# State scan of a fused GNN and Mamba kernel: where the exponentials lie, and which engine multiplies by B

## Chip, core and metric

The kernel runs on one core of a Trainium2 chip. The metric is the device time of one execution in microseconds (us). A core has TensorE (PE), VectorE (DVE), ScalarE (ACT) and GpSimd (POOL), which work in parallel and meet by semaphores, and a sync engine (SP) that issues transfers.

## What is computed

Two graph layers stand one behind the other. The second holds a selective state-space model (Mamba) over 4096 rows, with 256 channels and 16 states:

```python
dA = jnp.exp(dt[:, :, None] * A[None])
dBu = dt[:, :, None] * B[:, None, :] * u[:, :, None]

def step(hst, inp):
    dAt, dBut, Ct = inp
    hst = dAt * hst + dBut
    return (hst, hst @ Ct)
_, ys = lax.scan(step, jnp.zeros((D_INNER, D_STATE), h.dtype), (dA, dBu, C))
y = ys + u * D_skip
y = y * jax.nn.silu(z)
return y @ w_out
```

## The kernel before

Stage A, the first layer, comes first and is not touched. Stage B works on 8 tiles of 512 rows (`TILES`, `TILE`), numbered `b`. The 256 channels are two halves (`H`) of 128 partitions, so one state's sequence for a tile is 128 x 1024 elements, two halves side by side. Tile `b` has a **window** of 16 steps `n`, one for each state; in it the engines also prepare tile `b+1` (the "front") and finish tile `b-1` (the "tail"). Windows 0 and 1 and windows 6 and 7 are written out, 2 to 5 come out of a loop of two passes over two windows. Window 7 has a code of its own (`window_last`).

For a state `k` of a window:

- ACT writes the exponentials dA, one instruction for each half (L834), to SBUF (`dA`, 4 slots) or, for states in `IN_BANK` and the first half, to a PSUM bank (`dA_bank`, M1 being bank 3, or bank 6).
- dBu is the product of `dtu` and B. DVE makes it from a row of B that PE spread over the partitions in PSUM (`spread_B`, L1393, then L1111, into `dBuV`); for the states of `POOL`, GpSimd makes it from a copy of B that a transfer (`load_B`, L780, two states at a time into `b_sb`) has spread in SBUF (L546, into `dBuP`).
- DVE scans. A **banked** state takes two instructions, the first half from the bank (L1124), the second from SBUF (L1127); their start values are an operand. A **carried** state takes one instruction over both halves (L1132); its start value must stand in column 0 of the dBu tile, and ACT puts it there (`dBuP<-state`, L844), which DVE waits for (`start_set`). `AT['act_start']` = 1 puts that copy of state `k` into ACT's step `k+1`, behind the exponentials of that step.
- DVE multiplies by C (L1139, `pr`), from a bank that PE spread C into (`spread_C`, L1402), and PE adds the result up by transposing it into `yT` (`sum_state`, L1420).

Each engine runs its instructions in the order of its own list. `AT` is a table that says in which step `n` of an engine's list a piece of front or tail stands: `act_ax` (`front_ax`, L680, copies the finished product with the adjacency to SBUF), `act_g` (`front_relu`, L684), `act_fs` (`front_stats`, L691 to L698, mean and variance of the four row groups), `act_hn`, `act_skip` (`skip_term`, L759), `act_y` (`tail_copy`, L767, two copies that PE's sum of the next tile waits for), `pool_rs` (the power of -1/2 on GpSimd, L529). Within a step of ACT's list stand, in this order: the copy of the state four behind, the two exponentials, the start value, the load of B, the front, the skip term, the copies of y. DVE's step `n` holds the product with B of state `n`, the scan of state `n-1` and the product with C of state `n-2`. PE's step `n` holds the spread of B for state `n+1` (where DVE needs it), the sum of state `n-3`, a piece of the front and the spread of C for state `n-1`.

Of the kernel before, what the change touches and what calls it, by code (L numbers as in the profile page):

```python
# [7 lines left out]
ALU = mybir.AluOpType  # L8
ACT = mybir.ActivationFunctionType
# [16 lines left out]
S = 16  # L26
# [10 lines left out]
AT = dict(pool_rs=5, pool_tail_rs=13, dve_dt=14, act_hn=5, act_hT=6, act_silu=11, act_bc=13,
          act_sp=14, act_exp=14, act_ts=13, act_tail=15, dve_bc=11, dve_sp=14, dve_gate=1, pe_gcn=2, pe_gtr=3, pe_tr=6,  # L40
          pe_z=9, pe_dbc=10, pe_dt=11, pe_turn=2, pe_out=9, act_b0=15, act_ax=2, act_g=2, act_fs=4,
          act_start=1, act_skip=2, act_y=3)
FILL = (1, 1, 6, 1, 0, 0, 0, 9, 8)
CONV = (0, 0, 0, 0, 0, 0, 0, 4, 4, 0, 0, 0, 0, 0, 0, 0)
PLAN = (2, 4, 1, 2, 3, 3, 3, 0, 0, 0, 0, 2, 3, 3, 3, 3)
AHEAD = sum(PLAN[AT['pe_gcn']:])
C_IN_O = (0, 2, 4, 6)
POOL = (1, 2, 3, 4, 5, 6, 7, 9, 11, 13, 15)
IN_BANK = (1, 2, 3, 4, 5, 6)
CARRIED = tuple(k for k in range(S) if k not in IN_BANK)  # L50
B_LOADS = ((1, 2), (3, 4), (5, 6), (7, 9), (11, 13), (15,))
B_LOAD_AT = {3: 2, 5: 3, 8: 4, 11: 5}
POOL_AFTER = {n: 2 if n <= 7 else 3 for n in POOL}
SUM_AFTER = 3
LATE = (S - 2, S - 1)

# [1 line left out]
def gnn_mamba(nc, x, adj, x2, eps1, eps2, W1, b1, W2, b2, Wm, bm, gcn_w, gcn_b, ln_g, ln_b, w_in, conv_w,  # L58
              conv_b, w_xp, w_dt, b_dt, A_log, D_skip, w_out, out):
    POOL_B = POOL  # L60
    ctx = ExitStack()
    with ctx:  # L62
# [50 lines left out]
        state = sb("state", [P, S, H])  # L113
# [22 lines left out]
        B = ExitStack()  # L136
# [37 lines left out]
        bank = [yT[:, 0:TILE], yT[:, TILE:]]  # L174
# [101 lines left out]
        turns = {5: [("C", 1), ("C", 3), ("C", 5), ("C", 7), ("C", 8), ("B", 12), ("C", 11), ("C", 12), ("C", 14)],  # L276
                 6: [("B", 8), ("B", 10), ("C", 9), ("C", 10), ("B", 14), ("C", 13), ("C", 15)]}
        bank_of = {it: k for k in turns for it in turns[k]}
        dA_bank = {1: M1, 2: bank[6], 3: M1, 4: bank[6], 5: bank[6], 6: bank[6]}

        def spread_bank(kind, n):
            return M0 if (kind, n) == ("B", 0) else bank[4] if kind == "C" and n in C_IN_O else bank[bank_of[kind, n]]
# [1 line left out]
        def dve_slot(n, par):  # L284
            return (n - nB(n) + NVB * par) % 2

        def pool_slot(n, par):
            return (nB(n) + NPB * par) % 2

        def dBu(n, par):  # L290
            return dBuP[pool_slot(n, par)] if n in POOL_B else dBuV[dve_slot(n, par)]

        LAST = TILES - 1
        last_dA = ((bank[7], bank[6]), (M0, M1))
# [122 lines left out]
        def _(pool):  # L417
# [121 lines left out]
            def window(b, par, tail, front):  # L539
                for n in range(S):  # L540
                    if n in POOL_B:
                        load = nB(n) // 2
                        pool.wait_ge(b_in[load % 2], 16 * (len(B_LOADS) // 2 * b + load // 2 + 1))
                        wait(pool, scanned, S * b + n - POOL_AFTER[n] + 1 if n > 1 else S * b)
                        pool.wait_ge(dtu_ready, b + 1)
                        nc.gpsimd.tensor_tensor(dBu(n, par)[:, :, 1:], dtu[par][:, :, :],  # L546
                                                b_sb[load % 2][:, nB(n) % 2:nB(n) % 2 + 1, :].to_broadcast([P, H, TILE]),
                                                ALU.mult).then_inc(dBu_by_pool, 1)
                    if front and n == AT['pool_rs']:
                        front_rs(b + 1)  # L550
                    if tail and n == AT['pool_tail_rs']:
                        tail_rs(b - 1)
# [29 lines left out]
        def _(act):  # L582
# [233 lines left out]
            def window(b, par, tail, front):  # L816
                for n in range(S):
# [18 lines left out]
                    first = n - AT['act_start']
                    for k in range(first, S if n == S - 1 else min(first + 1, S - 1)):
# [98 lines left out]
        def _(dve):  # L936
# [167 lines left out]
            def window(b, par, tail, front):  # L1104
                for n in range(S + 2):
# [99 lines left out]
        def _(pe):  # L1205
# [390 lines left out]
```

## Time and profile before

| | us |
|---|---|
| median of 3 runs (1086.82 to 1090.28) | 1087.23 |
| the profiled execution's own time | 1086.18 |
| its span, first to last instruction | 1084.6 |
| DVE busy | 995.6 |
| PE busy | 971.7 |
| ACT busy | 559.5 |
| POOL busy | 337.6 |

The rows further down come from that one execution. Their first number is the start in us from the beginning of the span, the second the duration. What stands in brackets is idle time of the engine ahead of the row and what ended it. Since instructions of one engine overlap by some tenths of a us, the pace of a row is the distance to the next start, not the duration.

### The profile page before, as it was taken

The numbers are of one execution on the slowest core, as the hardware profiler recorded it, in microseconds if no ns is written. First come the engines' busy times: TensorE is split into PE (matmuls) and PEld (weight loads), VectorE is DVE, ScalarE is ACT, GpSimd is POOL, SyncE is SP. The second block draws the span as 40 slices with busy tenths as digits, with TensorE's granted clock in tenths as the row PEclk, the third lists the DMA queues.
The fourth block names the chain that finished last, engine by engine and source line by source line (L and its number), as shares of the span: only waits on it lengthen the run. The fifth ranks groups of instructions, "written<-read, shape, count | busy, mean of one in ns | idle before, by whom it ended". The sixth has DMA issues, their size and how long they took to land. (4 is left out here: it accounts for less than half of the span.)

```text
span 1084.6 us, 13272 instructions
## 1 busy us (share of the span) xinstructions
PE 971.7 (90%) x4134; PEld 671.6 (62%) x4134; DVE 995.6 (92%) x735; ACT 559.5 (52%) x1110; POOL 337.6 (31%) x228
## 2 busy tenths in 40 slices
PE   2889999999999999999998998989989999877665
PEld 2667777777777777634554564655646556445554
DVE  5989999999999999771999999999999999999996
ACT  3343343434343434225583875767847758477342
POOL 5450202020202021100532634426335263253652
PEclk9899999999999999999999999999999999988566
DMA  9999999999999999963825535365164452211200
GB/s 255 259 267 312 332 310 347 324 345 321 355 324 343 324 341 343 225 213 140 309 98 212 213 103 195 142 215 213 61 223 165 175 179 83 97 68 68 99 1 20
DMA packets 190396, 233.72 MB, mean 215 GB/s; under 512 B 8880, under 2 KB 164592, under 8 KB 175760
## 3 DMA queue, kind: packets, MB, share of 16 engines
q1 hardware_dynamic: 105936, 163.60, 46.3%
q10 hardware_dynamic: 80896, 60.57, 20.8%
q0 software_dynamic: 3520, 9.04, 2.8%
q8 instruction: 18, 0.29, 0.1%
q14 instruction: 26, 0.21, 0.1%
HBM read 170.00 MB, written 63.18 MB: 215 GB/s over the span
## 5 line engine op out<-in xcount | busy, mean ns | idle before, releaser
L958 DVE STREAM_TRANSPOSE at<-rows 128x1024 f32<-128x1024 f32 x136 | 267.8, 2011 | 21.9 <-DMA rows<-in_adj 7.5
L546 POOL TENSOR_TENSOR dBuP<-dtu,b_sb 128x1024 f32<-128x1024 f32 x77 | 182.9, 2376 | 282.1 <-DVE dtu L1074 115.1
L1223 PE MATMUL yT<-ah,xh 128*128 128x512 f32 x512 | 212.3, 415 | 34.8 <-DVE al L966 27.0
L599 ACT ACTIVATE ah<-at 128x2048 fp32r<-128x2048 f32 x64 | 122.6, 1915 | 211.4 <-PE yT L1223 196.1
L1310 PE MATMUL bank<-adjc,xm 128*128 128x512 f32 x448 | 206.0, 595 | 0.8 <-ACT axT L680 0.8
L1223 PE MATMUL yT<-al,xh 128*128 128x512 f32 x512 | 202.1, 395 | 0.0
L1223 PE MATMUL yT<-ah,xl 128*128 128x512 f32 x512 | 201.9, 394 | 0.0
L1420 PE MATMUL yT<-ident,pr 128*128 128x128 f32 x1008 | 147.4, 294 | 37.7 <-DVE pr L1139 31.2
L1420 PEld LDWEIGHTS yT<-ident,pr 128*128 128x128 f32 x1008 | 128.1, 152 | 67.9 <-DVE pr L1139 45.6
L834 ACT ACTIVATE dA<-dt,A_sb 128x512 f32<-128x512 f32 x182 | 122.6, 711 | 43.0 <-DVE dt L1071 43.0
L1139 DVE TENSOR_TENSOR pr<-hs,bank 128x1024 f32<-128x1024 f32 x112 | 134.3, 1199 | 11.2 <-PE bank L1402 11.0
L1223 PEld LDWEIGHTS yT<-ah,xh 128*128 128x128 f32 x512 | 97.8, 191 | 67.3 <-DVE al L966 34.0
L966 DVE TENSOR_TENSOR al<-at,ah 128x2048 fp32r<-128x2048 f32 x57 | 129.2, 2266 | 4.8 <-ACT ah L599 4.8
L1310 PEld LDWEIGHTS bank<-adjc,xm 128*128 128x128 f32 x448 | 81.2, 191 | 78.1 <-issue 77.3
L1223 PEld LDWEIGHTS yT<-ah,xl 128*128 128x128 f32 x512 | 97.7, 191 | 23.2 <-issue 3.6
L1223 PEld LDWEIGHTS yT<-al,xh 128*128 128x128 f32 x512 | 97.5, 190 | 21.2
L1132 DVE TENSOR_TENSOR_SCAN hs<-dA,zero,dBuV 128x1026 f32<-128x1026 f32 x35 | 83.0, 2371 | 1.8 <-ACT dA L834 1.4
L1132 DVE TENSOR_TENSOR_SCAN hs<-dA,zero,dBuP 128x1026 f32<-128x1026 f32 x35 | 83.9, 2397 | 0.0
L504 POOL TENSOR_TENSOR al<-at,ah 128x2048 fp32r<-128x2048 f32 x7 | 32.3, 4612 | 157.2 <-ACT ah L599 157.2
L1402 PE MATMUL bank<-bc,sel 128*128 128x512 f32 x112 | 73.9, 660 | 3.5 <-DVE pr L1139 1.8
L1127 DVE TENSOR_TENSOR_SCAN hs<-dA,state,dBuP 128x512 f32<-128x512 f32 x42 | 62.7, 1493 | 0.0
L1344 PE MATMUL bank<-hT,w_cv_sb 128*128 128x512 f32 x128 | 58.3, 599 | 0.2 <-ACT hT L713 0.2
(187 smaller groups left out, 1190.0 us busy)
## 6 DMA issues: line engine op xcount, KB each, us to landing
adjT<-at SPq DMA_DIRECT2D x56, 1024.0 KB, 7.5
adjc<-adjT SPq DMA_DIRECT2D x56, 1024.0 KB, 5.3
rows<-in_adj SPq DMA_DIRECT2D x152, 256.0 KB, 8.3
rows<-in_adj ACTq DMA_DIRECT2D x136, 256.0 KB, 8.7
b_sb<-b_dram ACTq DMA_DIRECT2D x37, 512.0 KB, 4.9
xm<-in_x SPq DMA_DIRECT2D x4, 512.0 KB, 10.7
res<-in_x POOLq DMA_DIRECT2D x8, 256.0 KB, 7.1
mid<-xn POOLq DMA_DIRECT2D x8, 256.0 KB, 7.9
```

Source lines behind the costliest of these rows:

```text
L546: nc.gpsimd.tensor_tensor(dBu(n, par)[:, :, 1:], dtu[par][:, :, :], b_sb[load % 2][:, nB(n) % 2:nB(n) % 2 + 1, :].to_broadcast([P, H, TILE ...
L599: nc.scalar.activation(ah[c % 2][:, :], at[c % 2][:, :, :].rearrange("p m t -> p (m t)"), ACT.Copy)\
L834: nc.scalar.activation(dA_bank[n][:, :] if n in IN_BANK and h == 0 else dA[n % NDA][:, h, 1:], dt_[par][:, h, :], ACT.Exp, scale=A_sb[:, h ...
L958: last = nc.vector.transpose(dst.rearrange("p m (g i) -> p g m i", i=32), src.rearrange("p g (i m) -> p g m i", i=32))
L966: nc.vector.tensor_tensor(al[c % 2][:, :], at[c % 2][:, :, :].rearrange("p m t -> p (m t)"), ah[c % 2][:, :], ALU.subtract).then_inc(chunk ...
L1127: nc.vector.tensor_tensor_scan(hs[k % NHS][:, 1, 1:], dA[k % NDA][:, 1, 1:], dBu(k, par)[:, 1, 1:], state[:, k, 1:2], ALU.mult, ALU.add).t ...
L1132: nc.vector.tensor_tensor_scan(flat[0], flat[1], flat[2], zero[:, :], ALU.mult, ALU.add)\
L1139: nc.vector.tensor_tensor(pr[k % NPR][:, :, :], hs[k % NHS][:, :, 1:], spread_bank("C", k)[:, :].unsqueeze(1).to_broadcast([P, H, TILE]), ...
L1223: last = mm(acc[k][:, :], w[:, b, :], v[c % 2][:, cols], start=(b == 0 and j == 0), stop=(b == KB - 1 and j == 2))
L1310: last = mm(accB[:, :], xm[:, b, :], adjc[c % NADJ][:, m, :], start=(b == 0), stop=(b == KB - 1))
L1402: mm(spread_bank("C", n)[:, :], sel[:, S + n:S + n + 1].to_broadcast([P, P]), bc[par][:, :], start=True, stop=True).then_inc(C_spread, 1)
L1420: m = mm(yT[:, DI * q + P * h:DI * q + P * h + P], src[:, h, P * q:P * q + P], ident[:, :], is_transpose=True, start=first and h == 0 and ...
```

## The change

Three of the banked states, 0, 2 and 4, read the exponentials of both halves from banks (M1 and bank 6). States 5, 6, 7 and 8 read the first half from bank 6. States 1 and 3, which were banked, become carried. GpSimd makes the product with B of state 8 too (12 of 16), so DVE and PE's spread are left with 0, 10, 12 and 14; the pairs of loads and the dBu slots are set anew. The product's wait is a table (`POOL_BEHIND`: the scan that product `n` stands behind). The power moves from behind product 5 to behind product 4, `front_stats` from ACT's step 4 to 3, the skip term from 2 to 1, the copies of y from 3 to 2.

```diff
-AT = dict(pool_rs=5, ... act_fs=4,
-          act_start=1, act_skip=2, act_y=3)
+AT = dict(pool_rs=4, ... act_fs=3,
+          act_start=1, act_skip=1, act_y=2)
...
-POOL = (1, 2, 3, 4, 5, 6, 7, 9, 11, 13, 15)
-IN_BANK = (1, 2, 3, 4, 5, 6)
+POOL = (1, 2, 3, 4, 5, 6, 7, 8, 9, 11, 13, 15)
+WHOLE_IN_BANK = (0, 2, 4)
+IN_BANK = (0, 2, 4, 5, 6, 7, 8)
...
-B_LOADS = ((1, 2), (3, 4), (5, 6), (7, 9), (11, 13), (15,))
-B_LOAD_AT = {3: 2, 5: 3, 8: 4, 11: 5}
-POOL_AFTER = {n: 2 if n <= 7 else 3 for n in POOL}
+B_LOADS = ((1, 2), (3, 4), (5, 6), (7, 8), (9, 11), (13, 15))
+B_LOAD_AT = {3: 2, 5: 3, 6: 4, 10: 5}
+POOL_BEHIND = {1: -1, 2: -1, 3: 1, 4: 1, 5: 3, 6: 3, 7: 5, 8: 6, 9: 7, 11: 8, 13: 10, 15: 12}
...
-        dA_bank = {1: M1, 2: bank[6], 3: M1, 4: bank[6], 5: bank[6], 6: bank[6]}
+        dA_bank = {(0, 0): M1, (0, 1): bank[6], (2, 0): M1, (2, 1): bank[6], (4, 0): bank[6], (4, 1): M1,
+                   (5, 0): bank[6], (6, 0): bank[6], (7, 0): bank[6], (8, 0): bank[6]}
...
         def dBu(n, par):
-            return dBuP[pool_slot(n, par)] if n in POOL_B else dBuV[dve_slot(n, par)]
+            if n in (2, 5):
+                return dBuV[1]
+            if n in POOL_B:
+                return dBuP[0 if n in (1, 4, 7, 9, 13) else 1]
+            return dBuV[dve_slot(n, par)]
...
-                        wait(pool, scanned, S * b + n - POOL_AFTER[n] + 1 if n > 1 else S * b)
+                        wait(pool, scanned, S * b + POOL_BEHIND[n] + 1)
...
-                        if n == 2:
-                            wait(act, C_multiplied, S * b)
-                        elif n == 3:
-                            act.wait_ge(half_scanned, len(IN_BANK) * b + 1)
-                        elif 4 <= n <= 6:
-                            act.wait_ge(half_scanned, len(IN_BANK) * b + (2 if n == 4 else n - 1))
+                        if n in (2, 4):
+                            act.wait_ge(scanned, S * b + n - 1)
+                        elif n in (5, 6, 7, 8):
+                            act.wait_ge(half_scanned, len(IN_BANK) * b + n - 2)
                         for h in range(H):
-                            nc.scalar.activation(dA_bank[n][:, :] if n in IN_BANK and h == 0 else dA[n % NDA][:, h, 1:], dt_[par][:, h, :], ACT.Exp,
+                            if n == 0 and h == 1:
+                                wait(act, C_multiplied, S * b)
+                            nc.scalar.activation(dA_bank[n, h][:, :] if (n, h) in dA_bank else dA[n % NDA][:, h, 1:], dt_[par][:, h, :], ACT.Exp,
...
-                            nc.vector.tensor_tensor_scan(hs[k % NHS][:, 1, 1:], dA[k % NDA][:, 1, 1:], dBu(k, par)[:, 1, 1:],
-                                                         state[:, k, 1:2], ALU.mult, ALU.add).then_inc(scanned, 1)
+                            nc.vector.tensor_tensor_scan(hs[k % NHS][:, 1, 1:], dA_bank[k, 1][:, :] if k in WHOLE_IN_BANK else dA[k % NDA][:, 1, 1:],
+                                                         dBu(k, par)[:, 1, 1:], state[:, k, 1:2], ALU.mult, ALU.add).then_inc(scanned, 1)
```

ACT's list ahead of the change, from the copies of y in step 3 to the exponentials of state 5 (`bank3` and `bank6` are PSUM, `dA0` to `dA3` the SBUF slots, `hn` and `ve` the statistics):

```order
L767 ACTIVATE y<-yT 128x512 [waits y_turned] x2
L821 ACTIVATE state<-hs0 128x2 [waits scanned]
L834 ACTIVATE bank6<-dt1,A_sb 128x512 [waits half_scanned,scanned]
L834 ACTIVATE dA0<-dt1,A_sb 128x512
L691 ACTIVATE hn,mr<-bank2 128x128 [waits h_turned,f_mean_scaled,g_turned]
L691 ACTIVATE hn,mr<-bank2 128x128 x3
L695 ACTIVATE hn,sq<-bank2,mr 128x128 [waits f_mean]
L695 ACTIVATE hn,sq<-bank2,mr 128x128 x3
L698 ACTIVATE ve<-sq,eps_ln 128x4 [waits f_squares]
L821 ACTIVATE state<-hs1 128x2 [waits scanned]
L834 ACTIVATE bank6<-dt1,A_sb 128x512 [waits half_scanned,scanned]
L834 ACTIVATE dA1<-dt1,A_sb 128x512
```

ACT's list with the change, from the exponentials of state 3 to the start value of state 3 (the last row):

```order
L837 ACTIVATE dA3<-dt1,A_sb 128x512 [waits scanned]
L837 ACTIVATE dA3<-dt1,A_sb 128x512
L783 DMA b_sb0<-b_dram 128x1024 [waits dBu_by_pool]
L694 ACTIVATE hn,mr<-bank2 128x128 [waits h_turned,f_mean_scaled,g_turned]
L694 ACTIVATE hn,mr<-bank2 128x128 x3
L698 ACTIVATE hn,sq<-bank2,mr 128x128 [waits f_mean]
L698 ACTIVATE hn,sq<-bank2,mr 128x128 x3
L701 ACTIVATE ve<-sq,eps_ln 128x4 [waits f_squares]
L824 ACTIVATE state<-hs0 128x2 [waits scanned]
L837 ACTIVATE bank6<-dt1,A_sb 128x512 [waits scanned]
L837 ACTIVATE bank3<-dt1,A_sb 128x512
L847 ACTIVATE dBuP1<-state 128x2 [waits state_kept,scanned]
```

The statistics now stand ahead of the exponentials of state 4, and behind these there is a start value for state 3, which had none.

DVE's list ahead of the change, from the second half of state 6 to the scan of state 7:

```order
L1127 SCALAR_TENSOR_TENSOR hs2<-dA2,state,dBuP1 128x512
L1139 TENSOR_TENSOR pr1<-hs1,bank5 128x1024 [waits summed,scanned,C_spread]
L1107 REGISTER_ALU
L1111 TENSOR_TENSOR dBuV1<-dtu0,bank6 128x2x512 [waits scanned,B_spread]
L1116 ISA
L1118 REGISTER_ALU [waits dA_ready]
L1130 REGISTER_ALU [waits C_multiplied,state_kept,dBu_by_pool]
L1132 SCALAR_TENSOR_TENSOR hs3<-dA3,zero,dBuP0 128x1026 [waits start_set]
```

With the change, from the same second half of state 6:

```order
L1129 SCALAR_TENSOR_TENSOR hs2<-dA2,state,dBuP1 128x512
L1141 TENSOR_TENSOR pr1<-hs1,bank5 128x1024 [waits summed,scanned,C_spread]
L1119 ISA
L1121 REGISTER_ALU [waits dA_ready]
L1127 SCALAR_TENSOR_TENSOR hs3<-bank6,state,dBuP0 128x512 [waits C_multiplied,state_kept,dBu_by_pool]
L1129 SCALAR_TENSOR_TENSOR hs3<-dA3,state,dBuP0 128x512
```

The product with B of state 8 is gone from DVE, and state 7 is two half scans.

## Rows read from the trace of the kernel before

**Rows 1.** The stretch of one window: PE, PEld, DVE, ACT, POOL busy, clock, DMA.
```profile
728.63:798.80 70.17, 65.38 (x296) 40.77 (x295) 68.68 (x51) 47.38 (x123) 29.69 (x15) 1.00 0.47 170
```
**Rows 2.** Timeline of DVE in that window.
```profile
728.63 1.21 DVE L1139 TENSOR_TENSOR pr<-hs,bank 128x1024 f32<-128x1024 f32 x1
729.77 1.22 DVE L1111 TENSOR_TENSOR dBuV<-dtu,bank 128x1024 f32<-128x1024 f32 x1
731.34 2.35 DVE L1132 TENSOR_TENSOR_SCAN hs<-dA,zero,dBuV 128x1026 f32<-128x1026 f32 x1 [0.36 <-ACT dA L834]
733.61 1.20 DVE L1079 TENSOR_TENSOR yg<-yT,sz 128x1024 f32<-128x1024 f32 x1
...
737.15 1.19 DVE L1139 TENSOR_TENSOR pr<-hs,bank 128x1024 f32<-128x1024 f32 x1
738.26 1.27 DVE L1124 TENSOR_TENSOR_SCAN hs<-bank,state,dBuP 128x512 f32<-128x512 f32 x1
739.45 1.31 DVE L1127 TENSOR_TENSOR_SCAN hs<-dA,state,dBuP 128x512 f32<-128x512 f32 x1
740.69 1.19 DVE L1139 TENSOR_TENSOR pr<-hs,bank 128x1024 f32<-128x1024 f32 x1
...
744.24 1.19 DVE L1139 TENSOR_TENSOR pr<-hs,bank 128x1024 f32<-128x1024 f32 x1
...
750.08 2.25 DVE L1127 TENSOR_TENSOR_SCAN hs<-dA,state,dBuP 128x512 f32<-128x512 f32 x1
...
764.33 1.22 DVE L1139 TENSOR_TENSOR pr<-hs,bank 128x1024 f32<-128x1024 f32 x1 [0.47 <-PE bank L1402]
...
772.89 1.22 DVE L1139 TENSOR_TENSOR pr<-hs,bank 128x1024 f32<-128x1024 f32 x1 [0.57 <-PE bank L1402]
```
**Rows 3.** Timeline of PE in that window.
```profile
737.01 1.04 PE L1440 MATMUL yT<-ident,yg 128*128 128x128 f32 x8
...
746.39 1.03 PE L1420 MATMUL yT<-ident,pr 128*128 128x128 f32 x8
...
754.70 0.50 PE L1393 MATMUL bank<-bc,sel 128*128 128x512 f32 x1 [0.34 <-DVE hs L1124]
755.04 1.03 PE L1420 MATMUL yT<-ident,pr 128*128 128x128 f32 x8
...
772.05 0.80 PE L1402 MATMUL bank<-bc,sel 128*128 128x512 f32 x1
```
**Rows 4.** Timeline of POOL in that window: the power, and product 6.
```profile
746.72 1.94 POOL L529 TENSOR_TENSOR rs<-ve,neg_half 128x4 f32<-128x4 f32 x1
748.88 2.37 POOL L546 TENSOR_TENSOR dBuP<-dtu,b_sb 128x1024 f32<-128x1024 f32 x1
```
**Rows 5.** Timeline of ACT in that window.
```profile
734.47 0.60 ACT L680 ACTIVATE axT<-bank 128x512 f32<-128x512 f32 x1 [3.19 <-PE bank L1310]
736.36 0.69 ACT L684 ACTIVATE gT<-bank,gcn_b_sb 128x512 f32<-128x512 f32 x1 [1.29 <-PE bank L1323]
...
739.49 1.06 ACT L767 ACTIVATE y<-yT 128x512 f32<-128x512 f32 x2
...
741.15 0.72 ACT L834 ACTIVATE dA<-dt,A_sb 128x512 f32<-128x512 f32 x1
741.76 0.27 ACT L691 ACTIVATE hn<-bank 128x128 f32<-128x128 f32 x1
...
744.67 0.19 ACT L821 ACTIVATE state<-hs 128x2 f32<-128x2 f32 x1
...
756.85 0.19 ACT L844 ACTIVATE dBuP<-state 128x2 f32<-128x2 f32 x1
```
**Rows 6.** Window 0, timeline of ACT: relu.
```profile
527.95 0.69 ACT L684 ACTIVATE gT<-bank,gcn_b_sb 128x512 f32<-128x512 f32 x1 [1.22 <-PE bank L1323]
```
**Rows 7.** Window 0, timeline of PE: the sum of state 2.
```profile
536.65 1.03 PE L1420 MATMUL yT<-ident,pr 128*128 128x128 f32 x8
```
**Rows 8.** Loads of B (`b_sb`), issue to landing, all 44.
```profile
DMA to landing us min/median/max: 3.1/4.7/8.4
```

More of the change, by code:

```diff
@@ L35, in wait @@
         eng.wait_ge(sem, value)
-AT = dict(pool_rs=5, pool_tail_rs=13, dve_dt=14, act_hn=5, act_hT=6, act_silu=11, act_bc=13,
+AT = dict(pool_rs=4, pool_tail_rs=13, dve_dt=14, act_hn=5, act_hT=6, act_silu=11, act_bc=13,
           act_sp=14, act_exp=14, act_ts=13, act_tail=15, dve_bc=11, dve_sp=14, dve_gate=1, pe_gcn=2, pe_gtr=3, pe_tr=6,
-          pe_z=9, pe_dbc=10, pe_dt=11, pe_turn=2, pe_out=9, act_b0=15, act_ax=2, act_g=2, act_fs=4,
-          act_start=1, act_skip=2, act_y=3)
+          pe_z=9, pe_dbc=10, pe_dt=11, pe_turn=2, pe_out=9, act_b0=15, act_ax=2, act_g=2, act_fs=3,
+          act_start=1, act_skip=1, act_y=2)
 FILL = (1, 1, 6, 1, 0, 0, 0, 9, 8)
@@ L276, in gnn_mamba @@
         turns = {5: [("C", 1), ("C", 3), ("C", 5), ("C", 7), ("C", 8), ("B", 12), ("C", 11), ("C", 12), ("C", 14)],
-                 6: [("B", 8), ("B", 10), ("C", 9), ("C", 10), ("B", 14), ("C", 13), ("C", 15)]}
+                 6: [("B", 10), ("C", 9), ("C", 10), ("B", 14), ("C", 13), ("C", 15)]}
         bank_of = {it: k for k in turns for it in turns[k]}
-        dA_bank = {1: M1, 2: bank[6], 3: M1, 4: bank[6], 5: bank[6], 6: bank[6]}
+        dA_bank = {(0, 0): M1, (0, 1): bank[6], (2, 0): M1, (2, 1): bank[6], (4, 0): bank[6], (4, 1): M1,
+                   (5, 0): bank[6], (6, 0): bank[6], (7, 0): bank[6], (8, 0): bank[6]}
         def spread_bank(kind, n):
@@ L285, in dve_slot @@
             return (n - nB(n) + NVB * par) % 2
-        def pool_slot(n, par):
-            return (nB(n) + NPB * par) % 2
         def dBu(n, par):
-            return dBuP[pool_slot(n, par)] if n in POOL_B else dBuV[dve_slot(n, par)]
+            if n in (2, 5):
[3 more added lines that the diff above has]
+            return dBuV[dve_slot(n, par)]
         LAST = TILES - 1
@@ L304, in last_dBu @@
         def last_dBu(n):
-            return (dBuV[1], dBuP[1], dBuV[0], dBuP[0])[n % 4]
+            return (dBuV[0], dBuP[0], dBuV[1], dBuP[1])[n % 4]
         def wait_low(eng, it, c):
@@ L1123, in window @@
                         if k in IN_BANK:
-                            last = nc.vector.tensor_tensor_scan(hs[k % NHS][:, 0, 1:], dA_bank[k][:, :], dBu(k, par)[:, 0, 1:],
-                                                                state[:, k, 0:1], ALU.mult, ALU.add)
-                            last.then_inc(half_scanned, 1)
-                            nc.vector.tensor_tensor_scan(hs[k % NHS][:, 1, 1:], dA[k % NDA][:, 1, 1:], dBu(k, par)[:, 1, 1:],
-                                                         state[:, k, 1:2], ALU.mult, ALU.add).then_inc(scanned, 1)
+                            nc.vector.tensor_tensor_scan(hs[k % NHS][:, 0, 1:], dA_bank[k, 0][:, :], dBu(k, par)[:, 0, 1:],
+                                                         state[:, k, 0:1], ALU.mult, ALU.add).then_inc(half_scanned, 1)
+                            nc.vector.tensor_tensor_scan(hs[k % NHS][:, 1, 1:], dA_bank[k, 1][:, :] if k in WHOLE_IN_BANK else dA[k % NDA][:, 1, 1:],
+                                                         dBu(k, par)[:, 1, 1:], state[:, k, 1:2], ALU.mult, ALU.add).then_inc(scanned, 1)
                     if k in CARRIED:
@@ L1332, in front_tr @@
                 pe.wait_ge(f_normed, RG * (a + 1))
-                wait(pe, half_scanned, len(IN_BANK) * (a - 1) + 3)
+                wait(pe, scanned, S * (a - 1) + 5)
                 for q in range(RG):
@@ L1375, in bank_free @@
                 i = turn.index((kind, n))
-                if (kind, n) == ("B", 8):
+                if (kind, n) == ("B", 10):
                     pe.wait_ge(half_scanned, len(IN_BANK) * (b + 1))
```

## The prediction

> **What bounds the kernel now.** I read the stretches of the scan stage first. A window takes 70.17 us, with DVE busy for 68.68 and PE for 65.38, ACT for 47.38 and POOL for 29.69 [rows 1]; So DVE is the bound with little to spare, and PE stands close behind it. The timeline of DVE then shows where it doesn't work at its own pace [rows 2]. The second half scan of state 5 takes 2.25 us where its neighbour takes 1.31. GpSimd's product 6 runs from 748.88 to 751.25 at that moment [rows 4], and the scan, which reads two tensors from SBUF, ends 1.08 after it. So a DVE instruction with two SBUF sources waits for a running GpSimd product. Product 6 came that late because the power of 1.94 us stood in front of it. The other loss is DVE's wait of 0.57 for C of state 9 [rows 2]: PE runs without a gap, but for 0.34, from its sum of state 2 at 746.39 to the end of that spread at 772.85 [rows 3]. In the middle of a window it is PE's list that DVE waits for, and what DVE saves there turns into a longer wait unless PE gets earlier too.
>
> I write t for the time from the start of `pr` of state 15 (728.63 before) and compare windows by it.
>
> **What it removes.** Per window: DVE's product of state 8, 1.14 (from 728.63 to 729.77 an instruction of its kind moves the list on by that much [rows 2]); the stall of 0.94 (2.25 less 1.31); on PE the spread of B for state 8 with its wait, 0.34 + 0.34 = 0.68 [rows 3]. A GpSimd product more costs POOL 2.37, and POOL is idle for 40 us of the window, so nothing.
>
> **The form of the scans.** A half from a bank moves DVE on by 1.19, one from SBUF by 1.24, a carried scan by 2.27 (731.34 to 733.61) [rows 2]. Before: 6 x 2.43 + 10 x 2.27 = 37.3. After: 3 x 2.38 + 4 x 2.43 + 9 x 2.27 = 37.3. That costs nothing. The half from a bank takes 1.27, that from SBUF 1.31 [rows 2]: the bank is, if anything, the quicker source. The Trainium skill (VectorE: DVE Perf Modes, "The TRN2 errata") gives PSUM sources 120 cycles of fixed time and SBUF sources 58, at 0.96 GHz, 0.065 us more for each half that moves to a bank; by that the four halves more would cost 0.26 a window. The trace does not agree, and I go by the rows.
>
> **What it adds.** State 3 becomes carried, and its start value stands in ACT's list behind the exponentials of state 4, and these behind the statistics, the exponentials of state 3, the copies of y, relu and ax. All that stands behind the exponentials of state 2, which now wait until scan 0 has read both banks. That chain, by rows:
>
> - DVE starts scan 0 at t = 2.71, as now (731.34). Its own exponential for the second half waits for `pr` of state 15 and is done by about t = 2.0, since bank 6 gets free at 1.2; that is hidden. Two halves end at 2.71 + 1.19 + 1.27 = 5.17.
> - ACT: exponentials of state 2 from 5.25, two times 0.61 (741.15 to 741.76 is the pace of one [rows 5]), the start value of state 1, 0.19 long [rows 5], at 6.48 to 6.67. DVE is ready for scan 1 at 5.09 + 1.11 = 6.20 and starts it at 6.8: a stall of 0.6.
> - ax at 6.57 (its input is there at 5.84 already), relu 1.89 later (734.47 to 736.36 [rows 5]) at 8.46. The copies of y need PE's turn of yg, whose end is 3.58 behind ax (738.05 less 734.47 [rows 3, 5]), so 10.15; the second copy, half of the 1.06 for both [rows 5], and the small copy of a state are through by 10.8.
> - Exponentials of state 3 from 10.8 to 12.05 by pace; statistics 2.91 (741.76 to 744.67 [rows 5]) to 14.96; small copy 0.09; exponentials of state 4, 1.23, to 16.28; start value 0.19 to 16.47; DVE starts scan 3 at 16.6.
>
> DVE without this would come to scan 3 at 6.8 + 2.27 + 1.11 (737.15 to 738.26) + 2.38 + 1.11 = 13.65. So it stands still for 2.9 us. Leave out every wait of ACT on PE but the 1.3 in front of relu, and the chain still needs 10.6 from scan 0's end, against the 8.5 that DVE needs.
>
> **Who waits for that.** `pr` of state 2 starts at 16.6 + 2.27 = 18.87, now at 15.61 (744.24 [rows 2]). PE's sum of state 2 starts at 18.87 + 1.3 = 20.17, now at 17.76 (746.39 [rows 3]): 2.41 later. From there PE needs 26.46 to the end of C 9, less 0.68: the spread ends at 45.95, now at 44.22. So `pr` of state 9 comes 1.73 later, at 45.99 instead of 44.26 [rows 2]. DVE alone would be there sooner: from `pr` 2 to `pr` 9 it takes 28.65 now, of which go the product of 1.14, the stall of 0.94, waits of 0.57 and 0.47 for C of states 9 and 7 [rows 2] and 0.1 of a shorter stall: 25.4, so 44.3. It waits 1.7 us for PE. What the change saves on DVE is given back there. Behind `pr` 9 both lists are as before: 70.17 [rows 1] less 44.26 to the next window.
>
> **Other edits.** The power finds `ve` at about 15, in the time that DVE stands still, done by 16.2: no cost. Product 7 needs the load of 7 and 8, issued when ACT's wait on the first half of state 4 is over, t = 21.3; with the median of 4.7 [rows 8] it lands at 26.0, when scan 5 is over (25.96): no cost, with 8.4 up to 3.7, of which some 1.2 is slack. The skip term goes into the time that ACT waits for scan 0's end: the exponentials of state 1 leave it free at 3.2. The last window's own code is touched only in slots and the skip term: 0.
>
> **The sum.** Windows 1 to 6: 6 x 1.73 = 10.4. Window 0 has no copies of y: relu at 527.95 [rows 6], then 0.6, 1.24, 2.91, 0.09, 1.23, 0.33 give scan 3 at 534.35 and `pr` 2's end, +2.27 +1.22, at 537.85, so PE's sum at 537.9 for 536.65 [rows 7]: +1.3 less the spread's 0.6 = 0.7. Together +11.1 on the profiled 1086.18: 1097.3. The median of the runs stands 1.05 above that execution, so 1098.3; I say 1098.
>
> **Rivals.**
> - *PE keeps pace.* Then only DVE's own terms count: +0.6 +2.9 -1.14 -0.94 -0.1 and both waits of 1.04 [rows 2] gone, +0.3 a window, +2, 1089. For it: PE's busy time is 65.4 of 70.2. Against it: the gapless stretch [rows 3]. With the waits as long as now it is +1.3 a window, 1096, inside my case. 0.12.
> - *ACT is in time* (the other side). The start value of state 3 comes before t = 13.65, for instance since the sequencer reaches it early. Then PE's sums begin with the copies of y, 1.2 earlier than now, and lose 0.68: `pr` 9 comes 1.9 earlier, 7 x 1.9 = 13, 1074. Since GpSimd is out of the way of DVE's scans, this is what the change is worth without the chain. The Trainium skill (GPSIMD Engine Reference, "Specifications") names the same contention, DVE instructions with two SBUF inputs. It decides from a stall of scan 3 under about 0.7 instead of 2.9; ACT's busy rows alone exceed that. 0.08.
> - *A further wait.* Product 7 late by 2 us beyond the slack, or the windows at the end, where TensorE's clock is lower, stretching PE's part: +1 a window on top, 1105. 0.1.
> - My forecast, 1092 to 1102: 0.7.
>
> A difference of 0.3% (3.3 us) is about what can be told from no change. Slower: 0.7 + 0.1 + 0.01; same 0.10; faster 0.09. The range leaves out the lower rival and the far end of the third: 1089 to 1103.
>
> **What would show it.** In each window DVE idle for 0.6 ahead of scan 1 and near 2.9 ahead of scan 3, both ended by ACT's copy into dBuP; no half scan of 2.2 us; waits for C together 1.5 to 2 us; windows of 71.9. If scan 3 has no stall, the ACT chain is wrong; if it has one and the windows are of 70.5, PE was no bound.

## The result, and the profile after

The median of 5 runs is 1095.23 us (1094.97 to 1098.98) against 1087.91 (1086.82 to 1090.28, 5 runs) of the kernel before: the ratio is 1.0066, its 95% interval 1.0047 to 1.0084. The whole interval lies above 1, so the change made the kernel slower, by 0.7%. The forecast was 1098 in a range of 1089 to 1103, with 0.81 on slower. The profiled execution took 1095.15, its span 1093.3, 8.7 more than before.

The stretch of one window after (window 3), from `pr` of state 15 to the next one's, columns as in [rows 1]:

```profile
735.71:807.17 71.46, 64.87 (x295) 40.59 (x294) 66.58 (x51) 47.36 (x122) 31.08 (x16) 1.00 0.48 170
```

DVE works 2.1 us less than before and the window takes 1.29 more. The timeline of DVE in that window shows why (to be laid beside [rows 2]):

```profile
735.71 1.21 DVE L1141 TENSOR_TENSOR pr<-hs,bank 128x1024 f32<-128x1024 f32 x1
...
738.31 1.28 DVE L1127 TENSOR_TENSOR_SCAN hs<-bank,state,dBuV 128x512 f32<-128x512 f32 x1 [0.26 <-DVE dBuV L1114]
739.51 1.26 DVE L1129 TENSOR_TENSOR_SCAN hs<-bank,state,dBuV 128x512 f32<-128x512 f32 x1
740.68 1.20 DVE L1082 TENSOR_TENSOR yg<-yT,sz 128x1024 f32<-128x1024 f32 x1
742.27 2.35 DVE L1134 TENSOR_TENSOR_SCAN hs<-dA,zero,dBuP 128x1026 f32<-128x1026 f32 x1 [0.38 <-ACT dBuP L847]
...
748.02 1.20 DVE L1141 TENSOR_TENSOR pr<-hs,bank 128x1024 f32<-128x1024 f32 x1
752.03 2.35 DVE L1134 TENSOR_TENSOR_SCAN hs<-dA,zero,dBuP 128x1026 f32<-128x1026 f32 x1 [2.82 <-ACT dBuP L847]
754.30 1.20 DVE L1141 TENSOR_TENSOR pr<-hs,bank 128x1024 f32<-128x1024 f32 x1
...
760.09 1.26 DVE L1129 TENSOR_TENSOR_SCAN hs<-dA,state,dBuV 128x512 f32<-128x512 f32 x1
...
772.70 1.22 DVE L1141 TENSOR_TENSOR pr<-hs,bank 128x1024 f32<-128x1024 f32 x1 [0.75 <-PE bank L1404]
...
781.27 1.22 DVE L1141 TENSOR_TENSOR pr<-hs,bank 128x1024 f32<-128x1024 f32 x1 [0.58 <-PE bank L1404]
```

Scan 3 (752.03) stands still for 2.82 us, until ACT has put its start value in; scan 1 (742.27) for 0.38. Scan 5's second half, 2.25 before, takes 1.26. The words "scan 3" and "C 9" stand for the scan of state 3 and for the spread of C for state 9, and t is the time from the start of `pr` of state 15. The sum of DVE's terms in this window: stalls +0.38 +2.82; the product with B of state 8, which is gone, -1.14; long half scan -0.94 to -0.99; the wait at scan 0 -0.36 +0.26; waits for C 0.75 + 0.58 = 1.33 for 1.04, +0.29. Together +1.3, as the windows say.

ACT's timeline shows what the start value of state 3 (751.81) stood behind:

```profile
740.80 1.30 ACT L837 ACTIVATE bank<-dt,A_sb 128x512 f32<-128x512 f32 x2 [0.49 <-DVE hs L1129]
742.04 0.19 ACT L847 ACTIVATE dBuP<-state 128x2 f32<-128x2 f32 x1
742.14 0.57 ACT L683 ACTIVATE axT<-bank 128x512 f32<-128x512 f32 x1
744.00 0.69 ACT L687 ACTIVATE gT<-bank,gcn_b_sb 128x512 f32<-128x512 f32 x1 [1.29 <-PE bank L1325]
745.29 1.08 ACT L770 ACTIVATE y<-yT 128x512 f32<-128x512 f32 x2 [0.61 <-PE yT L1442]
...
746.36 1.33 ACT L837 ACTIVATE dA<-dt,A_sb 128x512 f32<-128x512 f32 x2
747.59 0.27 ACT L694 ACTIVATE hn<-bank 128x128 f32<-128x128 f32 x1
...
750.29 0.30 ACT L701 ACTIVATE ve<-sq,eps_ln 128x4 f32<-128x4 f32 x1
...
750.59 1.28 ACT L837 ACTIVATE bank<-dt,A_sb 128x512 f32<-128x512 f32 x2
751.81 0.19 ACT L847 ACTIVATE dBuP<-state 128x2 f32<-128x2 f32 x1
```

From 740.80 on ACT waits for no more than 1.29 + 0.61 us; the rest is its own work. The exponentials of state 3 are done at 747.69, and what the copy of 0.19 still stands behind is 2.9 of statistics and 1.22 of exponentials for another state.

PE's timeline, where its sum of state 2 waits for `pr` of state 2, and the end of C 9's spread:

```profile
755.56 1.09 PE L1422 MATMUL yT<-ident,pr 128*128 128x128 f32 x8 [1.82 <-DVE pr L1141]
...
780.43 0.80 PE L1404 MATMUL bank<-bc,sel 128*128 128x512 f32 x1
```

The windows, from one `dtu` of DVE to the next (L1074 before, L1077 after), in us:

| window | 0 | 1 | 2 | 3 | 4 | 5 | 6 | sum |
|---|---|---|---|---|---|---|---|---|
| before | 71.70 | 70.19 | 70.14 | 70.16 | 70.14 | 71.23 | 71.41 | 494.97 |
| after | 72.66 | 73.13 | 71.57 | 71.46 | 71.58 | 71.47 | 70.77 | 502.64 |
| difference | +0.96 | +2.94 | +1.43 | +1.30 | +1.44 | +0.24 | -0.64 | +7.67 |

So 7.67 of the 8.7 us lie in the windows. The other 1.0 is +1.7 ahead of window 0 (its `dtu` starts at 517.21 instead of 515.47) and -0.7 behind window 6. The +1.7 need not be the change's: in before_blocks_later, whose code ahead of window 0 is that of before, this point lies at 517.40. Window 1 stands out. In PE's timeline there, the six adjacency matmuls that follow on the idle time take 4.27 us, the next six 2.74, as in the windows of the loop (2 to 5):

```profile
610.78 1.30 PE L1422 MATMUL yT<-ident,pr 128*128 128x128 f32 x8 [1.92 <-DVE pr L1141]
611.86 4.27 PE L1312 MATMUL bank<-adjc,xm 128*128 128x512 f32 x6
...
616.21 2.74 PE L1312 MATMUL bank<-adjc,xm 128*128 128x512 f32 x6
```

The view of stretches (columns as in [rows 1]) has the granted clock at 0.79 of the full 2.4 GHz over the first of these stretches and at 1.00 behind it (from 612 to 614 it is 0.50, the lower level of 1.2 GHz):

```profile
608.00:616.00 8.00, 6.08 (x18) 3.04 (x17) 8.00 (x7) 3.32 (x8) 4.68 (x2) 0.79 0.51 190
616.00:636.00 20.00, 20.00 (x105) 14.04 (x104) 17.82 (x15) 14.05 (x29) 9.51 (x4) 1.00 0.43 158
```

### The profile page after: what moved, and what is told of

It reads as the page before. It is cut to its first block and busy times, and to the rows that moved or that the text cites. A ratio compares the mean times of both kernels' runs of the same rounds, so it can differ in the third digit from the quotient of the medians.

```text
span 1093.3 us, 13226 instructions
## 1 busy us (share of the span) xinstructions
PE 967.3 (88%) x4127; PEld 668.0 (61%) x4127; DVE 981.6 (90%) x735; ACT 559.4 (51%) x1103; POOL 348.6 (32%) x235
## 5 line engine op out<-in xcount | busy, mean ns | idle before, releaser
L549 POOL TENSOR_TENSOR dBuP<-dtu,b_sb 128x1024 f32<-128x1024 f32 x70 | 166.0, 2376 | 250.5 <-DVE dtu L1077 115.1
L1134 DVE TENSOR_TENSOR_SCAN hs<-dA,zero,dBuP 128x1026 f32<-128x1026 f32 x42 | 99.6, 2372 | 23.3 <-ACT dBuP L847 23.3
L837 ACT ACTIVATE bank<-dt,A_sb 128x512 f32<-128x512 f32 x70 | 47.1, 685 | 128.6 <-DVE hs L1127 52.9
L837 ACT ACTIVATE dA<-dt,A_sb 128x512 f32<-128x512 f32 x154 | 103.1, 710 | 0.0
L1134 DVE TENSOR_TENSOR_SCAN hs<-dA,zero,dBuV 128x1026 f32<-128x1026 f32 x21 | 49.3, 2349 | 0.0
```

The source lines that it names most:

```text
L837: nc.scalar.activation(dA_bank[n, h][:, :] if (n, h) in dA_bank else dA[n % NDA][:, h, 1:], dt_[par][:, h, :], ACT.Exp, scale=A_sb[:, h, n ...
L1134: nc.vector.tensor_tensor_scan(flat[0], flat[1], flat[2], zero[:, :], ALU.mult, ALU.add)\
```

## The experiments

Each is one step away from a kernel named with it. A ratio is that of its median to the kernel before on the same chip, with the 95% interval; two experiments are compared by their ratios. The theory under test: ACT's list costs the 2.9 us at scan 3, and behind `pr` 2 it is PE's list that DVE waits for. The times of windows come from one profiled execution of each kernel.

### start_early: the start value ahead of the next exponentials

```diff
-          act_start=1, act_skip=1, act_y=2)
+          act_start=0, act_skip=1, act_y=2)
```

> The changed kernel, with the start value of a carried state one step earlier in ACT's list (behind its own exponentials, so ahead of the statistics for state 3). My theory: scan 3's stall of 2.8 us and scan 1's of 0.4 are gone, and then PE's list sets the pace: its sum of state 2 can start at t = 17.9 instead of 19.85 (its step 4 ends there), so a window shortens by 2.0 us, from 71.5 to 69.5, and the kernel takes 1081 us, with waits for C grown from 1.3 to over 3 us a window. Rival (DVE alone is the bound, PE has slack): a window shortens by the whole 3.2 us plus nothing in waits, 1073 us. Rival (the stall cost nothing, PE would be late anyway): 1095 us.

1084.27 us, 0.9945 [0.9913, 0.9976]. The stalls of scans 1 and 3 are gone. ACT's timeline has the start value of state 3 now ahead of the statistics:

```profile
743.09 0.20 ACT L847 ACTIVATE dBuP<-state 128x2 f32<-128x2 f32 x1
743.18 0.27 ACT L694 ACTIVATE hn<-bank 128x128 f32<-128x128 f32 x1
```

and DVE's timeline has scan 3 without a wait, and more waits for C (of states 6, 7 and 9):

```profile
744.25 2.45 DVE L1134 TENSOR_TENSOR_SCAN hs<-dA,zero,dBuP 128x1026 f32<-128x1026 f32 x1
...
761.63 1.22 DVE L1141 TENSOR_TENSOR pr<-hs,bank 128x1024 f32<-128x1024 f32 x1 [0.56 <-PE bank L1404]
...
766.17 1.22 DVE L1141 TENSOR_TENSOR pr<-hs,bank 128x1024 f32<-128x1024 f32 x1 [0.95 <-PE bank L1404]
...
774.74 1.22 DVE L1141 TENSOR_TENSOR pr<-hs,bank 128x1024 f32<-128x1024 f32 x1 [0.58 <-PE bank L1404]
```

So this one number turns 1.0066 into 0.9945: 1.2% of the time, some 13 us, hang on where a copy of 0.2 us stands in ACT's list. (The number moves the copies of all nine carried states, but in after only scans 1 and 3 waited for theirs.) Its windows 3 and 4, 69.35 and 69.46 us, lie 0.7 to 0.8 below those of before, as had been expected (69.5); all seven together lie only 4.2 below (490.77 for 494.97). The waits for C were expected at over 3 us and are 2.09 in window 3. The end of C 9's spread lies 43.41 behind `pr` 15, 0.81 less than the 44.22 of before, and 0.68 of that is the spread of B 8 that PE no longer makes. DVE has lost 2.1 us of work and waits 2.09 for C instead of 1.04: in this window what PE saves arrives in the time, the greater part of what DVE saves does not.

Something else takes a part of the gain. Without the stall of scan 3, GpSimd's product 7 waits 1.58 to 2.23 for its load in windows 0 to 5, and product 9 waits 2.64 to 2.96 for its own in windows 0, 1, 2 and 5; a half scan beside each is long. POOL's timeline in window 2 and, behind it, DVE's:

```profile
693.15 2.37 POOL L549 TENSOR_TENSOR dBuP<-dtu,b_sb 128x1024 f32<-128x1024 f32 x1 [2.86 <-DMA b_sb<-b_dram]
```

```profile
693.85 2.76 DVE L1129 TENSOR_TENSOR_SCAN hs<-dA,state,dBuP 128x512 f32<-128x512 f32 x1
```

The windows where product 9 is late take 71.87, 70.52, 70.22 and 70.80, those where it isn't 69.35, 69.46 and 68.55. start_blocks_load, below, comes back to these loads.

### stats_back: the statistics back where they stood

```diff
-... act_fs=3,
+... act_fs=4,
```

> The changed kernel, with the statistics back in ACT's step 4, behind the exponentials and the start value of state 3. My theory: it is the 2.9 us of statistics ahead of that start value that hold scan 3, whatever else moves; scan 3 stalls for 0.6 instead of 2.8, PE begins its sum of state 2 at t = 17.9, a window takes 69.5 to 69.8 us and the kernel 1081 to 1083 us. Rival (the chain is long anyway, by relu and the copies of y): the stall stays above 2 us and the time above 1092 us.

1084.12 us, 0.9951 [0.9926, 0.9976]. DVE's timeline in one window, scan 3:

```profile
745.42 2.35 DVE L1134 TENSOR_TENSOR_SCAN hs<-dA,zero,dBuP 128x1026 f32<-128x1026 f32 x1 [1.00 <-ACT dBuP L847]
```

The stall is 0.39 to 1.07 in its windows (0.6 expected). Moving the statistics away takes as much off the time as moving the copy ahead of them, and nothing but their place differs. The carried form alone doesn't make the long stall (this run), and neither do the earlier statistics once the copy stands ahead of them (start_early); it takes statistics and copy in the order that after has. The kernel before with only its statistics moved was not run. With the later statistics the power is later too, product 6 runs into scan 5 again, and its second half takes 1.77 to 1.97 in each window, so the 1.26 of after goes with the earlier statistics.

### start_more_dve: is DVE or PE the bound?

On start_early, a product with a bank (1.13 of pace) that nothing reads, ahead of `pr` of state 7:

```diff
+                        if k == 7:
+                            nc.vector.tensor_tensor(dBuV[0][:, :, 1:], dtu[par][:, :, :],
+                                                    spread_bank("C", k)..., ALU.mult)
```

> The kernel with early start values, and one product of DVE more per window, of the size of a product with B (1.1 us), ahead of the product with C of state 7, its result not used. It measures what such a product is worth at this place, as the one of state 8 that GpSimd took over. My theory: the waits for C of states 8 and 9 that follow (0.95 and 0.58 us) take it up, no change, 1084 us. Rival (DVE is the bound, each us on it counts): 7 x 1.1, 1092 us.

1087.11 us, 0.9978 [0.9966, 0.999]. DVE's timeline:

```profile
765.82 1.22 DVE L1142 TENSOR_TENSOR dBuV<-dtu,bank 128x1024 f32<-128x1024 f32 x1 [0.95 <-PE bank L1407]
766.96 1.21 DVE L1144 TENSOR_TENSOR pr<-hs,bank 128x1024 f32<-128x1024 f32 x1
...
774.86 1.19 DVE L1144 TENSOR_TENSOR pr<-hs,bank 128x1024 f32<-128x1024 f32 x1
```

The expectation was no change (1084), its rival 1092; the time lies between, and its interval overlaps that of start_early, so it is the windows that speak. The seven grow by 3.44 us together (490.77 to 494.21), 0.49 for each, where 1.13 was added; window 3 grows by 0.45 (69.35 to 69.80). The wait of 0.58 for C 9 swallows its length of it. The expectation had also counted the wait of 0.95, which it put at state 8: it is that of state 7, and the added product stands behind it. What this suggests: behind state 7 DVE has 0.6 of slack, then it is the bound, and neither engine has much room. The evidence is no stronger than that, since the late loads fall on other windows here than in start_early (product 9 waits for its load in windows 0, 3 and 4).

### PE's list: blocks_later, before_blocks_later, start_blocks, start_blocks_three

`PLAN` says how many blocks of the adjacency product stand in each step of PE's list. Two of them move out of the gapless stretch, from steps 5 and 6 to 14 and 15; done on after, on before and on start_early:

```diff
-PLAN = (2, 4, 1, 2, 3, 3, 3, 0, 0, 0, 0, 2, 3, 3, 3, 3)
+PLAN = (2, 4, 1, 2, 3, 2, 2, 0, 0, 0, 0, 2, 3, 3, 4, 4)
```

> The changed kernel, with one block of the adjacency product less in each of PE's steps 5 and 6 and one more in each of steps 14 and 15 (1.76 us of PE work moved out of the stretch that ends with C of state 9). My theory: the waits of DVE for C of states 7 and 9, 1.33 us a window, go, and nothing else does, since scan 3 still stalls: 1086 us. Rival (PE is a bound over the whole window, by its 65 us of work): the waits come back at states 13 to 15 and the time stays at 1095 us.

> The kernel before, with the same two blocks moved. My theory: its waits for C of 0.47 and 0.57 us go, in seven windows, 1080 us. Rival (the wait is only that of the start of the conv products, or the blocks are as dear at their new place): 1088 us.

> The kernel with the start values one step earlier, and the two blocks of PE's steps 5 and 6 moved to 14 and 15. There PE, not DVE, is late at its sums of states 3 and 4, so the moved work should bring the spreads of C forward. My theory after the first four runs: C of state 7 is no longer waited for (0.56 us), but PE's z product then waits for ACT's u, whose place is set by the exponentials, so the waits for C of states 8 and 9 stay in part; a window 0.5 to 1.0 us shorter than 69.4, 1079 us. Rival (PE's work alone sets the pace): 1.76 us shorter, 1071 us. Rival (PE's new idle time lowers its clock, as in the run on the kernel before): a window longer than 70 us.

On after: 1094.26 us, 1.0039 [1.0016, 1.0063], where the theory wanted 1086. On before: 1095.68, 1.0042 [1.0021, 1.0062], where it wanted 1080. Both are misses: the first can't be told from after (1.0066 [1.0047, 1.0084]), the second is slower than before. On start_early: 1077.45, 0.9888 [0.9857, 0.992], near the 1079 expected. PE's timeline of blocks_later shows why the first gains so little:

```profile
762.59 1.09 PE L1422 MATMUL yT<-ident,pr 128*128 128x128 f32 x8 [0.66 <-DVE pr L1141]
...
774.83 1.99 PE L1355 MATMUL bank<-w_in_sb,hT 128*128 128x256 f32 x8 [0.49 <-ACT u L727]
...
780.42 0.80 PE L1404 MATMUL bank<-bc,sel 128*128 128x512 f32 x1
```

With its list shorter by two blocks, PE waits 0.66 for DVE's `pr` 4 and 0.49 for ACT's `u`, and C 9 is spread at 780.42, against 780.43 with all blocks in. With scan 3 late by 2.8, three chains (DVE's, PE's, ACT's) end close to one another: take 1.76 us off PE's, and the other two hold C 9 at the same time. On before PE's timeline is another:

```profile
757.33 0.50 PE L1393 MATMUL bank<-bc,sel 128*128 128x512 f32 x1 [2.04 <-DVE hs L1124]
...
758.93 4.90 PE L1344 MATMUL bank<-hT,w_cv_sb 128*128 128x512 f32 x8
...
764.76 3.60 PE L1344 MATMUL bank<-hT,w_cv_sb 128*128 128x512 f32 x8
```

PE comes early to the spread of B 8 and waits 2.04 for its bank, which a half scan of DVE must leave first. The eight convolution matmuls behind it take 4.90 us instead of 3.60. The view of stretches for PE (length, PE busy, granted clock, DMA) shows the clock ahead, behind the wait, and later:

```profile
740.00:754.80 14.80, 14.55 (x77) 1.00 0.58 213
757.30:763.30 6.00, 5.97 (x18) 0.72 0.13 47
763.30:770.00 6.70, 6.70 (x34) 1.00 0.11 39
```

This happens in windows 2 to 6 (idle for 1.91 to 2.04 at that place, then 4.38 to 5.06 for the eight matmuls), and they take 71.80 to 72.01. In windows 0 and 1 the idle time is at most 1.63, the matmuls take 3.60, and these windows are shorter than before's: 71.42 for 71.70 and 69.48 for 70.19. So on before the moved blocks gain a little where PE's idle time stays short, and lose where it reaches about 2 us and the clock falls behind it.

On start_early neither obstacle stands in the way: scan 3 is in time and the spread of B 8 is gone. What is left there is, in PE's timeline, ACT's `u`:

```profile
764.63 1.99 PE L1355 MATMUL bank<-w_in_sb,hT 128*128 128x256 f32 x8 [0.60 <-ACT u L727]
```

A third block taken away as well, with steps 4 to 6 at (2, 2, 2) and 13 to 15 at (4, 4, 4):

> As the kernel with early start values and moved blocks, with one block more moved, from PE's step 4 to 13. Theory: PE's z product waits for ACT's u already, so nothing is gained: 1077 us, and where PE's idle time grows its clock may fall and the time rise to 1080 us or more. Rival (PE's work still sets the pace): 0.88 us a window, 1071 us.

1075.04 us, 0.9868 [0.9852, 0.9884], inside the interval of start_blocks, so no gain is shown, as expected: the waits for C of states 8 and 9 are 0.58 and 0.68 as with two (0.57 and 0.68), and PE waits longer for `u` (0.81 to 1.36 behind window 0, where start_blocks has 0.60 to 1.07).

### start_blocks_silu: ACT's `u` and gates a step earlier

```diff
-AT = dict(... act_silu=11,
+AT = dict(... act_silu=10,
```

> As the kernel with early start values and moved blocks, and u and the gates one step earlier in ACT's list (ahead of the exponentials of state 11). If ACT's u is what holds PE's z product, this gives the rest: waits for C under 1 us a window, windows of 68.0 us, 1073 us. If it isn't, no difference to the kernel without it.

1079.71 us, 0.9903 [0.9872, 0.9934]: no gain, where 1073 was expected. PE's wait for `u` is gone behind window 0, but DVE's timeline has another wait for ACT in its place, 1.11 to 1.16 at `bc` in each window, where start_blocks has 0.53 in window 0 and none behind it:

```profile
706.32 0.69 DVE L1060 TENSOR_TENSOR bc<-bank,bc 64x512 fp32r<-64x512 f32 x1 [1.16 <-ACT bc L739]
```

### start_power_back: does the power's place matter?

On start_early, the power of -1/2 again behind product 5:

```diff
-AT = dict(pool_rs=4,
+AT = dict(pool_rs=5,
```

> The kernel with early start values, and the power behind product 5 again. Products 6 then starts about 1 us later and runs into the second half scan of state 5, which takes 2.2 us again. My theory: DVE waits for PE at C of states 7 and 8 by 1.5 us in the same stretch, which takes up the 0.9 us: no change against the kernel with early start values, 1084 us, windows of 69.4. Rival (the stall adds up): 7 x 0.9, 1090 us.

1085.07 us, 0.9954 [0.9935, 0.9974], not to be told from start_early's 0.9945; in the two profiled executions the windows differ by 2.1 us together. Scan 5 was expected to take 2.2 us again, and it did not (1.37), so the run doesn't measure what that stall costs. Other half scans were long, for the reason that start_early has too. POOL's timeline:

```profile
753.93 2.39 POOL L549 TENSOR_TENSOR dBuP<-dtu,b_sb 128x1024 f32<-128x1024 f32 x1 [1.90 <-DMA b_sb<-b_dram]
...
762.87 2.39 POOL L549 TENSOR_TENSOR dBuP<-dtu,b_sb 128x1024 f32<-128x1024 f32 x1 [3.03 <-DMA b_sb<-b_dram]
```

and DVE's:

```profile
755.34 2.06 DVE L1129 TENSOR_TENSOR_SCAN hs<-dA,state,dBuP 128x512 f32<-128x512 f32 x1
...
763.30 3.04 DVE L1129 TENSOR_TENSOR_SCAN hs<-dA,state,dBuP 128x512 f32<-128x512 f32 x1
```

A product that starts late because its load is late falls onto a half scan that reads two tensors from SBUF. The scans end at 757.40 and 766.34, each 1.08 after the product's end at 756.32 and 765.26, as the long half scan of before did (752.33 and 751.25) [rows 2, 4], with a load as the cause here.

### start_blocks_load: the loads of B earlier

On start_blocks, the load of B for states 7 and 8 (pair 3) is asked for in ACT's step 4 instead of 5:

```diff
-B_LOAD_AT = {3: 2, 5: 3, 6: 4, 10: 5}
+B_LOAD_AT = {3: 2, 4: 3, 6: 4, 10: 5}
```

> The kernel with early start values and moved blocks, and the load of B for states 7 and 8 in ACT's step 4 instead of 5. There GpSimd's product 7 waits 1.5 us for that load, ends into the second half scan of state 6 and makes it 0.3 us longer (1.59 instead of 1.25). With the load earlier the wait and the 0.3 us go. Theory: what follows waits for PE at C of state 8 anyway, so the windows stay at 68.5 to 69 us and the time at 1077 us. Rival (it is on the path): 7 x 0.3, 1075 us, which the windows of the trace would show and the total hardly.

1073.47 us, 0.9865 [0.9843, 0.9887], the lowest time here, 1.35% below the kernel before; start_blocks_three (0.9868) can't be told from it. Its interval overlaps that of start_blocks too, but its windows don't behave like those: 70.11, 69.20, 68.31, 68.23, 68.29, 68.22, 68.25, where start_blocks has 68.25 to 70.58 with two of 70.16 and over behind window 0. Together they are 5.2 us shorter (480.61 for 485.80). So the theory (no gain, since DVE waits for PE behind it anyway) missed, and the rival's 0.3 a window was too small as well. In start_blocks POOL's timeline has product 7 waiting for its load, and in DVE's the second half scan of state 6 takes 1.59 beside it:

```profile
751.19 2.38 POOL L549 TENSOR_TENSOR dBuP<-dtu,b_sb 128x1024 f32<-128x1024 f32 x1 [1.52 <-DMA b_sb<-b_dram]
```

with the earlier load the same product waits for DVE alone, and the half scan takes 1.32:

```profile
749.30 2.39 POOL L549 TENSOR_TENSOR dBuP<-dtu,b_sb 128x1024 f32<-128x1024 f32 x1 [1.25 <-DVE hs L1129]
```

## Why the prediction held, point by point

- *The form of the scans costs nothing, and a bank is no slower source.* Right. In after a half from a bank moves DVE on by 1.20 (738.31 to 739.51) and the second by 1.17, against 1.24 from SBUF [rows 2].
- *The ACT chain.* Right in every link that the window read shows. Scan 1 waits 0.38 there (0.54 in windows 1 and 6, and 1.59 in window 0, for which the prediction had no term) for 0.6 forecast, scan 3 2.82 (2.75 to 2.93, 2.04 in window 6) for 2.9. start_early and stats_back show that this chain is the cause, each from its own side.
- *Who waits.* Right in kind. `pr` 2 starts at t = 18.59 (18.87 forecast), PE's sum of state 2 at 19.85 (20.17), C 9's spread ends at 45.52 (45.95), `pr` 9 starts at 45.56 (45.99). The window grows by 45.56 - 44.26 = 1.30, where 1.73 was the term. Of the 0.43 too much, 0.28 come from scan 3, which starts at 16.32 instead of 16.6: the exponentials of state 2 at the head of the chain start at 5.09 instead of 5.25, and scan 3 follows the start of its copy (16.10) by 0.22 instead of 0.32. The rest comes from PE's sum, 1.26 behind `pr` 2 for 1.3, and from its stretch, 25.67 long where 26.46 - 0.68 = 25.78 was the term.
- *Waits for C.* 1.5 to 2 was forecast, 1.33 is there in the windows of the loop, for the same reason.
- *The power and the long half scan.* Right: the power starts at 750.66, in DVE's idle time, takes 1.01 instead of 1.94, and no half scan of 2.2 is left in any window. Before, six windows had one, window 6 had none, and that of window 5 stood beside a product whose load was 2.46 late; the prediction took the stall for the power's in every window.
- *Load of 7 and 8: no cost.* Right: in after product 7 waits for DVE alone, since scan 3's stall gave the load time. start_early, start_power_back and start_blocks show what the cover was worth: without the stall product 7 waits 1.3 to 2.4 for its load in windows 2 to 5 and draws a half scan with it.
- *The sum.* 10.4 for windows 1 to 6 and 0.7 for window 0; measured 6.71 and 0.96. Several things lie behind it. Windows 2 to 4 have the smaller term (1.3 to 1.44). Windows 5 and 6 had more waits for C before (0.30, 0.86 and 0.57 in window 5; 0.32, 1.08, 1.05 and 0.58 in window 6), in whose place the new stall comes: +0.24 and -0.64, and window 6 of after waits 0.37 and 0.68 for C. Window 6 also runs at a lower clock in both kernels (granted clock 0.81 before, 0.82 after). I had taken all windows for alike, and this is the largest miss of the sum, 3.9 us. Against it stands window 1 with +2.94, 1.5 of it the slower adjacency matmuls. And 1.0 of the span's growth lies outside the windows, where I had put none. So the total came out nearer (8.7 of the profiled span for 11.1) than its parts: one miss of -3.9 and one of -1.0 against three of +1.2, +0.3 and +1.0, and that they offset one another in part is luck.
- *The bound.* "PE's list is what DVE waits for" was too simple. start_more_dve shows 0.6 of slack for DVE behind state 7, not more; blocks_later shows that with PE's list cut, DVE's `pr` 4 and ACT's `u` end as late. The forecast came out because the late `pr` 2 holds up every one of them.
- *Rival "PE keeps pace".* In its strict form it is out: it had both waits for C gone, and they grew from 1.04 to 1.33. Its milder form, with waits as long as now, gave +1.3 a window, which is what the loop's windows show, so the size alone does not decide between it and the forecast. The rows do as far as window 3 goes: PE has no idle time from its sum of state 2 at 755.56 to the end of C 9. blocks_later says that this list had little weight of its own, since C 9 ends at the same time without 1.76 us of it.
- *Rival "ACT is in time".* It forecast 1074. start_early is that case, and gives 1084: the rival took all seven windows for 1.9 shorter, and they became 0.6 shorter on average. It counted PE's sums as beginning 1.2 earlier and everything behind them as keeping up. In the two windows with little disturbance (3 and 4) only 0.7 to 0.8 arrive, and in four others the late load of product 9 takes even that. Two more moves, of PE's blocks and of one load, were needed to reach 1073; start_early with the load alone moved was not run.

What stays open: the earlier skip term and copies of y were in every kernel but those from before, and nothing here tells what they are worth. I did not try the 12 products without the new form of the scans either, so how much of start_early's 0.55% comes from GpSimd's product 8 and how much from the missing long half scan is worked out from timelines (0.68 of PE's spread in 0.81), not shown by a run.

## What to carry to other kernels

A copy of 0.2 us that another engine waits for must stand in its list as early as its inputs allow, ahead of work for later steps; when pieces of an in-order list are moved, add up all that then stands ahead of such a copy: here the carried form cost nothing that shows until the statistics stood ahead of its start value. Where the chains of several engines end within some tenths of a us of one another, work taken from one of them pays only as far as the others' lists get shorter too, so look at what each of them waits for after every step, loads included: here the stall hid a late load, and taking the stall away uncovered it. And repeat the sum for each window that is written out: waits that it already has cover part of a new delay.

## What the runs showed of the hardware

- A half scan with two SBUF sources that meets a running GpSimd product ends 1.08 us after that product, whenever it began: so in before, twice in start_power_back, and in start_blocks (753.06 + 1.59 = 754.65, the product 751.19 + 2.38 = 753.57). The profiled executions of the twelve kernels have 77 half scans of this kind that take over 1.4 us, and each ends 1.07 to 1.09 behind a product. The longest takes 3.21 (in start_more_dve) instead of 1.31. Half scans whose first source is a bank keep their length beside a product: in after those at 745.65 and 746.85 take 1.28 and 1.26 while products run from 744.70 to 749.43. The power on GpSimd takes 1.01 with DVE idle and 1.94 beside its scan [rows 4].
- PE idle for 1.92 (window 1 of after) and 2.04 us (window 3 of before_blocks_later) was followed by matmuls 1.5 and 1.3 us longer for the same work, in stretches whose granted clock is 0.79 and 0.72 in the mean, part of them thus at the lower level of 1.2 GHz. An idle time of 1.82 in the loop's windows was not: the six matmuls behind it took 2.74, at a clock of 1.00. But the length of the idle time alone does not decide. In window 0 of blocks_later and of start_blocks_three PE waits for `u` ahead of the same eight matmuls:

```profile
558.17 3.68 PE L1355 MATMUL bank<-w_in_sb,hT 128*128 128x256 f32 x8 [1.95 <-ACT u L727]
```

```profile
556.70 1.99 PE L1355 MATMUL bank<-w_in_sb,hT 128*128 128x256 f32 x8 [2.71 <-ACT u L727]
```

Behind 1.95 the granted clock is 0.56 (558.1 to 562), behind 2.71 it is 1.00 (556.7 to 562). What decides between the two outcomes these rows don't settle. Where the clock fell, a stall of PE of about 2 us cost 1.6 to 1.8 times its length, an estimate from the first two cases. The Trainium skill (TensorE: Matmul & The Clock Gate, "Why this matters for your kernels") says that an idle gap of PE between bursts of matmuls, if it is long enough, brings the lower level back. The trace agrees that the falls come behind idle time, but not on the length: the gap of 2.71 left the clock up where shorter ones brought it down.
